# Attention and feed-forward in one stream: K stacked by quarters, the logarithm of the row sums by bits and a series

## What is computed

```
x = x + layernorm(attention(layernorm(x)))      # 16 heads of 32, causal, ALiBi slopes, low-rank Q and KV
x = x + layernorm(rms(ffn(layernorm(x))))       # gate/up 512 -> 2 x 1408, silu, down 1408 -> 512
scores = q @ k.T / sqrt(32) - slope * |i - j|,  masked above the diagonal
attn = softmax(scores);  out = attn @ v
w = fp4_table[nibble] * scale_of_its_group_of_128        # gate_up and down
```

## Time and profile before

| | |
|---|---|
| three runs | 2530.64, 2532.10, 2532.20 us, median 2532.1 |
| profiled execution, its own time | 2531.45 us |
| its span | 2528.9 us |
| TensorE matmul busy | 2439.4 us, 96% of the span, 13372 instructions |
| TensorE weight load busy | 1116.3 us, 44% |
| VectorE busy | 1525.8 us, 60% |
| ScalarE busy | 1464.9 us, 58% |
| GpSimd busy | 602.6 us, 24% |
| mean granted TensorE clock | 0.985 of full |
| ScalarE table loads | 65, of 1283 ns each |

### The profile page before, as it was taken

One profiled execution on the slowest core, in us unless ns is written; L12 is line 12 of the kernel. 1 busy time (PEld: TensorE's weight loads), 2 busy tenths in 40 slices (PEclk: granted clock), 3 DMA queues, 4 the chain that ended last, 5 costly groups with the idle time before them and its releaser, 6 DMA issues.

```text
span 2528.9 us, 38723 instructions
## 1 busy us (share of the span) xinstructions
PE 2439.4 (96%) x13372; PEld 1116.3 (44%) x13372; DVE 1525.8 (60%) x4299; ACT 1464.9 (58%) x3927; POOL 602.6 (24%) x650
## 2 busy tenths in 40 slices
PE   6689999999999999999999999999999999999988
PEld 3334444444444444444444444444444444444433
DVE  6856466565646657475666647556564665757442
ACT  3656657475664747567474655747566474756610
POOL 5311312122131222313122131312313122231312
PEclk9699999999999999999999999999999999999999
DMA  5011120301212020121201112120121202012000
GB/s 145 13 34 40 43 59 27 75 19 35 51 43 59 18 71 14 51 51 35 67 18 55 31 51 51 35 68 18 40 46 43 59 24 74 15 41 51 19 16 17
DMA packets 99521, 108.89 MB, mean 43 GB/s; under 512 B 22895, under 2 KB 73199, under 8 KB 99311
## 3 DMA queue, kind: packets, MB, share of 16 engines
q1 hardware_dynamic: 98462, 105.65, 15.9%
q10 hardware_dynamic: 864, 0.79, 0.1%
HBM read 38.49 MB, written 16.78 MB: 22 GB/s over the span
## 4 chain that ended last, share of the span: by engine, by line
PE 83%; DVE 5%; SPq 4%; ACT 4%; issue 2%; DMA 1%; POOL 0%; POOLq 0%; DVEq 0%
PE dense L350 60%; PE psO L550 7%; SPq L307 4%; PE score L534 4%; PE low L517 3%; PE psO L350 3%; PE score L517 3%; PE low L534 1%; DMA kst<-arena 1%; DVE arena L897 1%; ACT L662 1%; ACT L735 1%; ACT low L656 1%; ACT arena L735 1%; DVE late L998 1%
## 5 line engine op out<-in xcount | busy, mean ns | idle before, releaser
L350 PE MATMUL dense<-arena,wgu 128*128 128x512 f16 x4224 | 997.4, 379 | 0.9 <-DVE arena L897 0.9
L350 PEld LDWEIGHTS dense<-arena,wgu 128*128 128x128 f16 x4224 | 404.2, 97 | 430.8 <-issue 7.6
L350 PE MATMUL dense<-wdn,arena 128*128 128x512 f16 x2112 | 533.0, 380 | 2.6 <-POOL arena L1163 2.6
L1163 POOL TENSOR_TENSOR arena<-late,arena 128x512 f16<-128x512 f32 x176 | 203.3, 1155 | 1060.6 <-DVE arena L931 1060.6
L1071 DVE CUSTOM_DVE_ANT_0 low<-low,mmax 128x128 f32<-128x128 f32 (+3 forms) x672 | 278.1, 435 | 269.2 <-PE low L517 267.3
L735 ACT ACTIVATE arena<-score 128x512 f32<-128x512 f32 (+3 forms) x720 | 302.0, 440 | 173.9 <-PE score L534 128.0
L656 ACT ACTIVATE low<-low,ncol 128x128 f32<-128x128 f32 (+3 forms) x672 | 299.7, 446 | 161.5 <-DVE ncol L1071 155.1
L656 ACT ACTIVATE score<-score,ncol 128x384 f32<-128x384 f32 x352 | 214.0, 608 | 151.4 <-DVE ncol L1071 151.0
L350 PEld LDWEIGHTS dense<-wdn,arena 128*128 128x128 f16 x2112 | 199.1, 98 | 186.8 <-issue 11.4
L1071 DVE CUSTOM_DVE_ANT_0 score<-score,mmax 128x384 f32<-128x384 f32 x352 | 214.1, 648 | 101.1 <-PE score L517 99.7
L534 PE MATMUL score<-qst,kst 128*128 128x512 f16 (+3 forms) x784 | 218.0, 305 | 18.4 <-ACT arena L735 17.1
(11 more groups left out here) (146 smaller groups left out, 2893.8 us busy)
## 6 DMA issues: line engine op xcount, KB each, us to landing
qst<-arena SPq DMA_DIRECT2D x384, 64.0 KB, 2.1
kst<-arena SPq DMA_DIRECT2D x186, 128.0 KB, 2.6
xin<-x SPq DMA_DIRECT2D x16, 1024.0 KB, 5.1
late<-x SPq DMA_DIRECT2D x64, 256.0 KB, 2.8
out<-late SPq DMA_DIRECT2D x64, 256.0 KB, 2.0
qst<-mrow SPq DMA_DIRECT2D x96, 8.0 KB, 1.9
wgu<-wo_t SPq DMA_DIRECT2D x1, 1024.0 KB, 13.2
wgu<-wq_down SPq DMA_DIRECT2D x1, 768.0 KB, 4.5
```

The source lines that it names most:

```text
L350: ins = nc.tensor.matmul(dst, w, a, start=first and k == 0, stop=last and k == len(tt) - 1)
L1163: nc.gpsimd.tensor_tensor(ht[:, 1, m, :], tb[:, m % 2, :], ht[:, 0, m, :], ALU.subtract).then_inc(sem["hl"], 1)
```

## The change

K is waited for by quarters: heads 4g + a for a = 0 to 3 have a semaphore each, the DMAs go quarter by quarter, and TensorE waits for quarter a ahead of the first tile of head a. `F_FIRST` falls from 35 to 24. The logarithm becomes: a guess from the bits of the sum (one multiplication and addition on the float read as an integer), the exponential of its negative on ScalarE, and a series in sum times exponential less 1. The first half's guess, series and split are GpSimd's, in slot 16 (16 operations); the second half's are VectorE's, in slots 41 and 42 (13 operations where there were 5). ScalarE's `log_sums` becomes `inverse_guess`, in slots 16 and 41. In step 0 the low half of Wo is one VectorE operation ahead of the first unit, 4 units stand ahead of slot 0 and the others at every second slot to 56, the Wdown decoding in slot 15, and 18 units instead of 14 have their high half from ScalarE.

```diff
-LN_SPLIT, LN_ROWS, LN_COPY = (18, 42), (19, 43), (20, 44)
+LN_SUMS, LN_SPLIT, LN_ROWS, LN_COPY = (16, 41), (16, 42), (19, 43), (20, 44)
-FIRST_UNITS = 9
-UNIT_SLOT = [-1] * FIRST_UNITS + [17 * k // 10 for k in range(UNITS - FIRST_UNITS)]
+FIRST_UNITS = 4
+UNIT_SLOT = [-1] * FIRST_UNITS + [2 * k for k in range(UNITS - FIRST_UNITS)]
+DOWN_SLOT = 15
-ACT_UNITS = [u for u in range(UNITS) if (u % RING < 2 if u < FIRST_UNITS else u % RING == 0)]
+ACT_UNITS = [u for u in range(UNITS) if u < FIRST_UNITS or u % 2]
-F_FIRST = 35
+F_FIRST = 24
-LN_AT = (16, 40)
+LN_AT = (16, 41)
...
+        def stack_k(queue, a):
+            for slot, s in enumerate((0, 0, 1)):
+                queue.dma_start(
+                    kst[HD * slot:HD * slot + HD, :, :].rearrange("p (g a) l -> p g a l", a=HG)[:, :, a, :],
+                    qk[HD * a:HD * a + HD, 2 + s, :, :]).then_inc(sem[f"kst{a}"], 16)
...
                 def maximum(k):
                     h, i = k // NT, k % NT
+                    if i == 0 and h < HG:
+                        pe.wait_ge(sem[f"kst{h}"], val(f"kst{h}", t, 48))
...
-                pe.wait_ge(sem["kstk"], val("kstk", t, 192))
                 pe.wait_ge(sem["qstk0"], val("qstk0", t, 192))
...
-                def log_sums(part):
-                    act.wait_ge(sem["rowsum"], val("rowsum", t, HALF * (part + 1)))
-                    nc.scalar.activation(lcol[:, HALF * part:HALF * part + HALF], scol[:, HALF * part:HALF * part + HALF],
-                                         ACT.Ln).then_inc(sem["ln"], 1)
+                def inverse_guess(part):
+                    act.wait_ge(sem["guess"], val("guess", t, part + 1))
+                    nc.scalar.activation(mh32[:, part, :], lcol[:, HALF * part:HALF * part + HALF], ACT.Exp,
+                                         scale=-1.0).then_inc(sem["ln"], 1)
...
                         taken(act, t, j["K"] + NG - 1)
-                        stack(nc.scalar, kst, 2, (0, 0, 1), 0, NG, range(2, HG), "kstk")
+                        for a in (1, 3):
+                            stack_k(nc.scalar, a)
...
                 if isinstance(t, int) and t == 0:
+                    act.wait_ge(s_wo_lo, 1)
                     for u in units_of(-1):
                         unit(u)
...
+                def guess_logs(part):
+                    dve.wait_ge(sem["rowsum"], val("rowsum", t, HALF * (part + 1)))
+                    nc.vector.tensor_scalar(lcol[:, at], scol[:, at].bitcast(i32), LN2 * 2.0 ** -23, 0.03 - 127 * LN2,
+                                            ALU.mult, ALU.add).then_inc(sem["guess"], 1)
+                def finish_logs(part):
+                    dve.wait_ge(sem["ln"], val("ln", t, part + 1))
+                    link(t, nc.vector.tensor_tensor(u, u, w, ALU.mult))
+                    link(t, nc.vector.tensor_tensor(log, ncol[:, at], log, ALU.subtract))
+                    linked(t)
+                    link(t, nc.vector.tensor_scalar(w, u, -1.0, None, ALU.add))
...
+                    for c in (-0.5, 1.0):
+                        link(t, nc.vector.scalar_tensor_tensor(u, u, c, w, ALU.add, ALU.mult))
+                        linked(t)
...
+                if isinstance(t, int) and t == 0:
+                    dve.wait_ge(s_raw_hi, 4)
+                    nc.vector.scalar_tensor_tensor(wo[:, 1, :, :].rearrange("p a b -> p (a b)"), raw[:, 9 * D:13 * D],
+                                                   S_W, wo[:, 0, :, :].rearrange("p a b -> p (a b)"),
+                                                   ALU.mult, ALU.subtract).then_inc(s_wo_lo, 1)
...
-                    pool.wait_ge(s_raw_hi, 4)
-                    flat = raw[:, 9 * D:13 * D]
-                    nc.gpsimd.tensor_scalar(flat, flat, S_W, None, ALU.mult).then_inc(s_wo_s, 1)
-                    pool.wait_ge(s_wo_s, 1)
-                    nc.gpsimd.tensor_tensor(wo[:, 1, :, :].rearrange("p a b -> p (a b)"), flat,
-                                            wo[:, 0, :, :].rearrange("p a b -> p (a b)"), ALU.subtract).then_inc(s_wo_lo, 1)
...
+                    if slot == LN_SUMS[0]:
+                        guess_logs(0)
+                        finish_logs(0)
```

More of the change, by code:

```diff
@@ L48 @@
     "po": (0, 0, 4, 4), "out0": (16, 0, 32, 32), "out1": (16, 0, 32, 32), "tanh": (0, 0, 11, 11), "hh": (0, 0, 11, 11),
[1 row of a table removed]
+    "hl": (0, 0, 11, 11), "chain": (8, 23, 60, 52), "guess": (0, 2, 2, 2), "series": (0, 14, 14, 14),
 }
@@ L1077, in step @@
                             unit(u)
[L1078 removed]
+                    if isinstance(t, int) and t == 0 and slot == DOWN_SLOT:
                         decode_down()
[L1080 to L1082 removed]
+                    if slot == LN_SUMS[1]:
+                        guess_logs(1)
+                    if slot == LN_SPLIT[1]:
+                        finish_logs(1)
                     for e in exp_tiles:
```

104 lines of the change are left out of this document (75 added, 29 removed), and 3 rows, old and new, of the table COUNTS.

## The result

| | before | after |
|---|---|---|
| runs | 4 | 4 |
| median | 2531.47 us | 2503.41 us (2500.34 to 2504.47) |
| ratio of the medians | | 0.9887, 95% interval 0.987 to 0.9904 |
| profiled execution, its own time | 2531.45 us | 2504.12 us |
| its span | 2528.9 us | 2502.4 us |

The change makes the kernel 28 us faster, 1.1%. The forecast was 33 us, 2499 us, with a range of 2488 to 2517.

What follows compares the result with a forecast made beforehand. TensorE was taken to bound the steady steps, VectorE most of the first step. Second log 13.9, less 1, K 5.2 and first step 15 sum to 33 us: 2499 us, range 2488 to 2517.

Steps and rivals of the forecast that it cites:

- The second log: Steady steps: without the logarithm's two table loads, TensorE's 15 waits for ScalarE's exponentials go, 13.9 us.
- the deduction of 1 us: Second half's logarithm: VectorE's longer split might delay TensorE's transpose; 1 us deducted over all steps, bounds 0 and 5.
- The first log: First half of each step: removed loads gain nothing; GpSimd's 15 operations at 0.38 us each stay hidden, cost 0.
- (b): GpSimd's series partly late at 0.44 to 0.58 us an operation, up to 2.1 us a step: 2500 to 2532; chance 0.11.
- (c): Each GpSimd series operation costs 0.63 us, the result 2.8 us late in 16 steps: 2544 us; chance 0.07.
- K: Steady steps: waiting for K by quarters removes TensorE's waits for the DMAs that stack K, 5.2 us.
- TensorE's products only change places: Step of the K forecast: fewer dense products ahead of the slots only moves them; no cost was charged.
- Its own refutation: TensorE idle for over 5 us in a steady stretch as long as the one with 15.6 would refute the steady part.
- The first step up to the slots: Wo's work moved to VectorE and 4 early units instead of 9 bring the first tile forward 10.3 us, to 48.9.
- The first step in the slots: Less VectorE work up to slot 22 gives 5 us net; after slot 23 net 0, bounds -3 and +6.
- Rival (a): First step gives little: late units and half clock eat the earlier start; 2509 to 2514 us; chance 0.15.

Runs made afterwards that it cites:

- r5_series23: The changed kernel with the second split operation of GpSimd's series made nine times instead of once, 23 operations instead of 15: 2529.24 us.
- r8_keepfirst: The changed kernel with `F_FIRST` = 35 and, in the first step, GpSimd's causal zeroing ahead of the slot's unit instead of behind it: 2494.70 us.
- r9_firstdve: r8_keepfirst with the first half's logarithm series also on VectorE, in the first step alone: 2495.99 us.
- r10_laterows: r8_keepfirst with TensorE's transpose of the second half's row sums and the copy two slots later in all steps: 2520.03 us.
- r1_f35: The changed kernel with 35 instead of 24 dense products ahead of slot 0: 2502.70 us.

## Why the prediction was right, and where it was off

Faster, by the mechanisms named, inside the range. Its terms one by one:

- **The second log, forecast 13.9 less 1.** With K's wait out of the way the logarithm is worth 1.00 us a step (149.42 to 148.42), 15.0 us in 15 steps, and alone on the kernel before 1.04 x 15 = 15.6. The stall of the earlier trace rows with 0.17 us added to the idle time was the right size or a little small, and the deduction of 1 us wasn't due: TensorE's transpose never waited for VectorE's series in a steady step.
- **The first log, forecast 0 with 0.44 us of room for an operation.** Right: 0.35 us, no wait. I had taken 0.38 between bounds of 0.33 and 0.63. The room was 1.8 us where the prediction's numbers give 0.9. The rivals (b) and (c) fall on this one number, and r5_series23 shows that they were priced in the right kind.
- **K, forecast 5.2, bounds 3.5 and 5.2.** Measured 0.26 x 15 = 3.9 us, and 4.0 on the medians, inside the bounds. The price of a stall was right: the 0.17 us added to each is there in 8 steps of 8. What was missing with K alone is the 1.3 us that stay with no wait for K, in part as waits for VectorE; why they stay isn't known.
- **"TensorE's products only change places": this step failed.** It was said of the 11 products that `F_FIRST` moves, and it is true of TensorE. But the end of the second down product moved with them by a slot, so GpSimd's root had to wait longer, and behind the root stood the zeroing. It costs 0.24 us a step, 3.6 us. In its paragraph on K the prediction asked what is queued behind a moved step for SyncE alone. Its own refutation, over 5 us of idle TensorE in the steady stretch, was met by a hair (5.1 us), and rightly so: 5.0 of it are this wait.
- **The first step up to the slots, forecast 10.3.** Measured 10.1 (49.04 for 48.9). The 4.95 and 4.63 us fell to 1.62 and 0.88, as forecast. Two small errors cancel in the sum: the first unit came 5.5 us earlier (46.37 for 51.83) and not 6.2, and the four units took 0.67 us each and not 0.82. That VectorE waits here for GpSimd's whole instruction is borne out by the mask; the OR, which ends 0.26 us before GpSimd's multiplication, was slowed and not held to its end.
- **The first step in the slots, forecast 5 net: this failed too.** It gave 1. The wait for GpSimd's series was 3.3 us and not 1.5; that for VectorE's series, 2.9 us, was not forecast; and the late units were charged to ScalarE and TensorE, 0 net, while it was GpSimd's order that they held up, 7.0 us of waits for the zeroing. r8_keepfirst shows that the last is the one that counted: 8 us, with the clock. The prediction left the clock as it is, by a mean of 0.56 that it gave for 59 to 160 us; the earlier trace rows has 0.56 for 59 to 105 alone, and 0.89 for 130 to 160. r9_firstdve and r10_laterows show that the other two were hardly lost time.

In sum, steady 18.1 forecast and 15.4 measured (14.4 and the 1.0 of the last part; by the terms 15.0 + 3.9 - 3.6 = 15.3), first step 15 forecast and 11.2 measured. The logarithm's 1.1 us more and the deduction of 1 us that wasn't due hid a part of what the new wait took. Rival (a), the first step giving little as its late units and the clock eat the earlier start, described what happened at the end of the first step, to 4 us of it and not to 10 or more. Both misses lie in the order of GpSimd, the engine with 24% busy time: I priced what it does and not who stands behind it.

Three things stay open: what moves the runs of r1_f35 by up to 8 us, how much of the gain of r8_keepfirst is the clock's, and why the parts of the first step give 15.6 us alone and 11.2 together.

## What to carry to other kernels

When a block of work is moved by a slot, write down for every engine what is triggered by its end and what stands behind that in the engine's order, even where the order itself doesn't change; an engine at 24% is no exception, and here it cost 3.6 us in the steady steps and 8, with the clock, in the first. Choose the engine of a small chain by what is queued behind it and not by its speed: the series takes twice as long on GpSimd and is free there, and on VectorE it costs 27 us. A wait in the trace is worth its time only if what follows isn't waiting for another engine too: two of the three kinds of wait in the first step's slots could be shortened without any gain.

## What the runs showed of the hardware

VectorE's series in the first step, in the timeline of VectorE of the kernel after: the same product that takes 0.19 us elsewhere takes 0.92 here.

```profile
114.97 0.92 DVE L982 TENSOR_TENSOR scol<-scol,mh 128x32 f32<-128x32 f32 x1
```

GpSimd, in its timeline, works from 114.79 to 115.85:

```profile
114.79 1.06 POOL L1187 TENSOR_TENSOR arena<-late 128x512 f32<-128x512 fp8e4 x1 [1.52 <-PE dense L391]
```

VectorE's operation ends at 115.89, 0.04 us after it. In a steady step the first product of the series (1153.49, 0.60 us for 0.19) ends at 1154.09, 0.04 us after a zeroing of GpSimd (1153.41, 0.64 us). So a small operation too is held until GpSimd's is done; in a chain of 0.22 us steps, one such meeting costs two to three steps. How long it runs on behind GpSimd's end goes with its columns. Two rows of the kernel before, of VectorE and of GpSimd, show it for 512 columns, 0.28 us:

```profile
304.05 0.74 DVE L978 TENSOR_SCALAR late<-late,rs_lo,ve_lo 128x512 f32<-128x512 f32 x1
```

```profile
303.88 0.64 POOL L1176 TENSOR_SCALAR_AFFINE_SELECT arena<-arena 128x512 f32<-128x512 f32 x1
```

The traces of all runs here have over 1100 VectorE operations of up to 512 columns that took clearly longer than the same ones alone. Every one overlaps an operation of GpSimd and ends behind it: by 0.01 us on 1 column, 0.02 on 4, 0.04 on 32, 0.28 on 512 with one input (0.54 alone) and 0.54 with two (0.69 alone). The Trainium skill, page "SBUF — State Buffer", section "SBUF: two separate sides", calls the shared port pair an exclusive lock held for the whole instruction, and these rows agree with it. The OR of the first step, which ends ahead of GpSimd's multiplication, is the one case seen here that doesn't.

Small operations on GpSimd (128x32, fp32) take 0.22 to 0.37 us and follow each other, each waiting for the last, after 0.35 us on the mean; those of VectorE take 0.18 us and follow after 0.22 us. Powers cost more: 0.55 to 0.79 us on one column and 1.01 to 1.05 us on four.
